# Second graph layer: the input scaling moves from GpSimd to ScalarE, tile by tile, three streams behind the powers

## The chip, the core and the metric

The kernel runs on one core of one Trainium2 chip. The number that counts is the device time in microseconds (us) of one execution. The names of the engines in the rows are PE (TensorE matmul), PEld (TensorE weight load), DVE (VectorE), ACT (ScalarE), POOL (GpSimd) and SP (SyncE, which issues most DMAs).

## What is computed

The input x has 128 graphs of 128 nodes with 128 features, and adj holds a 128 x 128 matrix for each graph. Four blocks follow one another, each added to its own input:

```python
x = x + _L0_gnn_ref(_layernorm(x), adj, ...)    # attention over the graph
x = x + _L0_ffn_ref(_layernorm(x), ...)         # 30 steps: tanh, silu, layernorm, 128x128 product
x = x + _L1_gnn_ref(_layernorm(x), adj, ...)    # relu(f @ W[:d] + (adj @ f) @ W[d:] + bias)
x = x + _L1_ffn_ref(_layernorm(x), ...)         # 8 experts, top 2 of them for each row
```

`_layernorm(x)` is `(x - mean) / sqrt(var + 1e-5)` over the 128 features. The change touches the one in front of the third block, the second graph layer. Its mean is folded into the weights, so that only a multiplication of each row by `1/sqrt(var + eps)` is left.

## The kernel before

The 128 graphs are cut into 16 streams (`STREAMS`) of 8 graphs (`TILES`). A stream's tensor is 128 partitions by 8 tiles by 128 values in float32: `resid[s]` holds what the blocks are added to, `values[s]` (the first 128 columns of `state[s]`) what is being worked on. Every engine has its own program, written out by hand as a software pipeline: in slot k an engine works on stream k of one stage, stream k-1 of the next, and so on. Each engine executes strictly in the order of its program, and semaphores join the engines. No scheduler moves anything.

The 30 steps of the second block run as a loop over 16 slots each. Behind the loop comes its **tail** (`iteration(STEPS, tail=True)`), in which the streams that are still in flight are finished. In slot k of the tail:

- PE transposes a stream (`flip`, L1084), if k is at most 12, and then forms `rows` (L1090 the bias, L1094 the product with `w_ffn`), if k is at most 13. In slot k, `rows` needs the stream that was flipped in slot k-1. The flip of slot k waits for `x2_ready` of k, that is, for DVE's addition in slot k-1, since it writes the PSUM banks which that addition reads.
- ACT copies the stream flipped in slot k-1 out of PSUM into `turned` (L957), and PE's `rows` of slot k waits for this copy.
- DVE adds the product of PE's slot k-2 to `resid[k]` (L691, `x2_ready`), takes the statistics (L661) and writes the variance `x_var` (L665, `x2_var_ready`). DVE has 16 such slots.
- POOL has no part of its own in the tail. Its program goes from the last multiplication of the loop (L515) on to 30 small constant instructions (L524 to L543) and then to the loop over 16 streams at L547 to L552: the power -1/2 of the variance (`rsqrt`, L485, raises `x2_pow`), the multiplication of all 8 tiles by it in one instruction (L550, raises `x2_scaled`), and a copy of row numbers (L552).

Then comes the **second graph layer**, `for k in range(GNN1_SLOTS)` on PE, DVE and ACT. In slot k, PE waits for `x2_scaled` of stream k and flips `values[k]`; it forms the product Q of stream k-1 with `w_mix` (L1094), the mix of stream k-2 (two products for each tile, L1094), flips stream k-4 of the layer's output and forms its router logits (L1213). ACT copies the flip of stream k out (L1021, T below), then the product Q of stream k-1 (L1024), then statistics (L1027) and the flip of stream k-4 (L1032). PE's product Q of stream b waits until ACT has copied out the one of b-1 (`q_copied`). At first POOL has nothing else to do; then it scatters the finished rows to DRAM (L556, 128 indirect DMAs), a stream at a time, when DVE has found their places (L835). The fourth block works on the sorted rows when all are scattered.

Of the kernel before, what the change touches and what calls it, by code (L numbers as in the profile page):

```python
# [10 lines left out]
ALU = mybir.AluOpType  # L11
ACT = mybir.ActivationFunctionType
# [6 lines left out]
def network(nc, x, adj, W_w, W_b, a_w, a_b, ln_w, ln_b, F_W, F_b, G_w, G_b,  # L19
# [4 lines left out]
    TILES = 8  # L24
    STREAMS = B // TILES
    ITERS = 30
    STEPS = STREAMS * ITERS
# [33 lines left out]
    with ExitStack() as ctx:  # L61
        def sb(name, shape, dt=F32):
            return ctx.enter_context(nc.sbuf_tensor(name, shape, dt))

        def sem(name):
            return ctx.enter_context(nc.semaphore(name))
# [27 lines left out]
        resid = [resid_all[:, s] for s in range(STREAMS)]  # L94
        state = [sb(f"state{s}", [P, TILES, ROW]) for s in range(STREAMS)]
        values = [t[:, :, 0:D] for t in state]
# [7 lines left out]
        x_var = [sb(f"x_var{j}", [P, TILES]) for j in range(4)]  # L104
        x_rstd = [sb(f"x_rstd{j}", [P, TILES]) for j in range(4)]
# [8 lines left out]
        minus_half = sb("minus_half", [P, TILES])  # L114
# [150 lines left out]
        x2_pow = sem("x2_pow")  # L265
        x2_scaled = sem("x2_scaled")
# [57 lines left out]
        def wide(v, n=D):  # L324
            return v.unsqueeze(2).to_broadcast([P, v.shape[1], n])

        def halves(v):
            return v.rearrange("p (i h) -> p i h", h=2)

        def of_stats(t, which):  # L330
            return t[:, :, :].rearrange("p i (h e) -> p i h e", h=2)[:, :, :, which]
# [18 lines left out]
        SILU_LAG, STATS_LAG, SCALE_LAG, FLIP_LAG, EVAC_LAG = 1, 2, 5, STREAMS - 3, STREAMS - 2  # L350
        POOL_TILES = 6

        PEEL_FROM, PEEL_EACH = STREAMS + 2, 3
        PEELED = PEEL_EACH * (GNN0_SLOTS - PEEL_FROM)
        Q_LAG, MIX_LAG, X3_LAG, ROWS_LAG, ROUTE_LAG, RANK_LAG, PLACE_LAG = 1, 2, 3, 4, 5, 6, 7
        GNN1_SLOTS = STREAMS + PLACE_LAG
        def not_first(i):
# [5 lines left out]
        def in_flight(k, *lags):  # L363
            return [k - lag if 0 <= k - lag < STREAMS else None for lag in lags]

        def stages(lags, k, base, peeled, tail):
            for lag in lags:
                j = k - lag
                if tail and j >= 0 or peeled and j < 0:
                    yield None, None  # L370
                else:
                    yield base + j, j % STREAMS
# [91 lines left out]
        def _(pool):  # L464
# [19 lines left out]
            def rsqrt(dst, src, done, n):  # L484
                nc.gpsimd.tensor_tensor(dst, src, minus_half[:, 0:src.shape[1]], ALU.pow).then_inc(done, 1)  # L485
                pool.wait_ge(done, n + 1)
# [49 lines left out]
            for low in range(NE - 1):  # L536
# [4 lines left out]
                last = low == NE - 2  # L541
# [3 lines left out]


            for s in range(STREAMS):  # L547
                pool.wait_ge(x2_var_ready, s + 1)
                rsqrt(x_rstd[s % 4][:, :], x_var[s % 4][:, :], x2_pow, s)
                nc.gpsimd.tensor_tensor(values[s], resid[s], wide(x_rstd[s % 4][:, :]), ALU.mult  # L550
                                        ).then_inc(x2_scaled, 1)
                nc.gpsimd.tensor_copy(state[s][:, :, TOKEN].bitcast(I32), ids[:, s * TILES:(s + 1) * TILES])  # L552

            def scatter(s, tiles):
# [8 lines left out]
            for k in range(STREAMS + SCATTER_LAG):  # L563
                s, m = in_flight(k, 0, SCATTER_LAG)
# [44 lines left out]
        def _(dve):  # L609
# [145 lines left out]

            iteration(0, peeled=True, slots=range(PEELED, STREAMS))
            with dve.Fori(STREAMS, STEPS, STREAMS) as q:
# [193 lines left out]
        def _(act):  # L951
            def iteration(base, peeled=False, tail=False, slots=range(STREAMS)):
                for k in slots:
                    (n, s), (l, v) = stages([EVAC_LAG, SILU_LAG], k, base, peeled, tail)
                    if n is not None:
                        act.wait_ge(it_flip, n + 1)
                        nc.scalar.copy(turned[s % 4], ring[s % 4]).then_inc(it_turned, 1)  # L957
                    if peeled:
                        if k >= 4:
                            act.wait_ge(state_read, k - 3)  # L960
                        nc.scalar.activation(turned[k % 4], values[k], ACT.Tanh).then_inc(tanh_done, 1)
                    elif not tail:
                        act.wait_ge(product, base + (k - STREAMS + 1))
                        nc.scalar.activation(values[k], ring[k % 4], ACT.Tanh).then_inc(tanh_done, 1)  # L964
                    if l is not None:
                        act.wait_ge(state_read, l + 1)
                        nc.scalar.activation(values[v], values[v], ACT.Silu).then_inc(silu_done, 1)  # L967
# [37 lines left out]
            act.wait_ge(h0_ready, STREAMS)  # L1005
            iteration(0, peeled=True, slots=range(PEELED, STREAMS))
            with act.Fori(STREAMS, STEPS, STREAMS) as q:
                iteration(q)
            iteration(STEPS, tail=True, slots=range(EVAC_LAG))


            for k in range(GNN1_SLOTS):
                a, b, f, e, r = in_flight(k, 0, Q_LAG, ROWS_LAG, ROUTE_LAG + 1, X3_LAG + 1)
                if e is not None:
                    act.wait_ge(centred_logits, e + 1)
                    nc.scalar.activation(parts[e % 4][:, :, :], parts[e % 4][:, :, :], ACT.Exp).then_inc(exps, 1)
                if a is not None:
                    act.wait_ge(x2_flip, a + 1)
                    if a >= 3:
                        act.wait_ge(mix_psum, a - 2)  # L1020
                    nc.scalar.copy(turned[a % 3], psF).then_inc(x2_turned, 1)  # L1021
                if b is not None:
                    act.wait_ge(q_psum, b + 1)
                    nc.scalar.copy(values[b], psQ).then_inc(q_copied, 1)  # L1024
                if r is not None:
                    act.wait_ge(x3_stats_done, r + 1)
                    nc.scalar.copy(halves(state[r][:, :, MEAN]), of_stats(x1_stats[r % 4], 1)).then_inc(columns_ready, 1)  # L1027
                if f is not None:
                    act.wait_ge(r_flip, f + 1)
                    if f >= 1:  # L1030
                        act.wait_ge(logit_psum, f)
                    nc.scalar.copy(turned[3], psF).then_inc(r_turned, 1)  # L1032
# [281 lines left out]
```

## Time and profile before

| | us |
|---|---|
| median of 3 runs | 2552.14 (2551.59 to 2553.27) |
| the profiled execution, its own time | 2566.49 |
| its span in the trace | 2564.7 |
| busy in it: PE / DVE / ACT / POOL | 2378.7 / 2081.9 / 1811.9 / 2027.5 |
| mean granted clock of TensorE | 0.969 of full speed |

The profiled execution took 14.35 us more than the median of the runs. All times of rows below are of the profiled one, counted from the start of its span. A busy engine is not the same as one that sets the time: the engines wait for one another through semaphores, and only the wait that ends last in a slot matters.

### The profile page before, as it was taken

How to read it: one execution, taken by the hardware profiler on the slowest of the kernel's cores; microseconds unless marked ns; L12 is line 12 of the kernel's file. 1: busy time of each engine (PE TensorE's matmuls, PEld its weight loads, DVE VectorE, ACT ScalarE, POOL GpSimd, SP SyncE). 2: the span in 40 equal slices, each digit the busy share in tenths (PEclk: the TensorE clock that was granted, in tenths of full speed). 3: DMA queues.
4: the chain of work that ended last, by engine and by line, in shares of the span. 5: the costliest groups of instructions: out<-in, count | busy, mean ns of one | idle time of the engine just before them, and what ended most of it. 6: DMA issues, size and time to landing. Idle time of an engine off the chain costs nothing.

```text
span 2564.7 us, 60894 instructions
## 1 busy us (share of the span) xinstructions
PE 2378.7 (93%) x19678; PEld 2320.6 (90%) x19935; DVE 2081.9 (81%) x5761; ACT 1811.9 (71%) x2185; POOL 2027.5 (79%) x1592
## 2 busy tenths in 40 slices
PE   6829999999999999999999999999862999999998
PEld 5829999999999999999999999989861999999998
DVE  5999999999999999999999999987572444444443
ACT  3779999999999999999999999833210334344333
POOL 4769999999999999999999999995764444444443
PEclk9969999999999999999999999999885999999999
DMA  9100000000000000000000000003223555555554
GB/s 261 69 1 1 0 0 0 0 0 0 0 0 0 0 0 0 0 0 0 0 0 0 0 0 0 0 18 110 75 73 109 212 216 212 211 214 216 212 212 148
DMA packets 121574, 164.56 MB, mean 64 GB/s; under 512 B 14982, under 2 KB 74018, under 8 KB 121360
## 3 DMA queue, kind: packets, MB, share of 16 engines
q1 hardware_dynamic: 111792, 145.12, 16.6%
q0 software_dynamic: 9088, 17.14, 2.0%
q10 hardware_dynamic: 608, 1.30, 0.2%
q8 instruction: 37, 0.61, 0.1%
q14 instruction: 49, 0.40, 0.0%
HBM read 40.40 MB, written 24.65 MB: 25 GB/s over the span
## 4 chain that ended last, share of the span: by engine, by line
DVE 58%; PE 31%; issue 7%; POOL 1%; DMA 1%; ACT 1%; SPq 1%; another core or an unknown queue 0%; DVEq 0%; POOLq 0%; ACTq 0%
DVE pair_stats L661 25%; DVE state L704 18%; PE psum L1265 11%; PE psum L1256 11%; DVE state L683 6%; PE psum L1094 5%; PE psum L1084 2%; DVE it_vars L665 2%; DVE x_stats L661 1%; POOL sorted_rows L556 1%; DVE resid L731 1%; PE psum L1213 1%; DMA sorted_rows<-state,slot 1%; PE psum L1246 1%; DVE state L700 1%
## 5 line engine op out<-in xcount | busy, mean ns | idle before, releaser
L1094 PEld LDWEIGHTS psum<-w_ffn,turned 128*128 128x128 f32 x7680 | 1010.1, 192 | 36.0
L1094 PE MATMUL psum<-w_ffn,turned 128*128 128x128 f32 x7680 | 1013.7, 275 | 12.8 <-issue 0.2
L512 POOL TENSOR_TENSOR it_rstd<-it_vars,minus_half 128x8 f32<-128x8 f32 x480 | 785.5, 1636 | 0.0
L515 POOL TENSOR_TENSOR state<-state,it_rstd 128x768 f32<-128x768 f32 x480 | 708.0, 1475 | 37.6
L661 DVE BATCH_NORM_STATS2 pair_stats<-state 128x6 f32<-128x256 f32 x1920 | 685.1, 418 | 0.0
L1084 PE MATMUL psum<-ident,state 128*128 128x128 f32 x4352 | 595.6, 281 | 59.1 <-DVE state L700 42.8
L704 DVE SCALAR_TENSOR_TENSOR state<-state,psum 128x1024 f32<-128x1024 f32 x464 | 560.8, 1209 | 1.8 <-ACT state L964 0.9
L1084 PEld LDWEIGHTS psum<-ident,state 128*128 128x128 f32 x4352 | 479.5, 143 | 78.0 <-issue 57.7
L957 ACT COPY turned<-psum 128x1024 f32<-128x1024 f32 x480 | 485.8, 1012 | 80.4 <-PE psum L1084 43.9
L967 ACT ACTIVATE state<-state 128x1024 f32<-128x1024 f32 x480 | 512.7, 1068 | 28.6 <-DVE state L700 9.1
L964 ACT ACTIVATE state<-psum 128x1024 f32<-128x1024 f32 x464 | 481.0, 1037 | 0.0
L1044 ACT ACTIVATE adjT<-psum 128x512 f32<-128x512 f32 x312 | 186.3, 597 | 283.3 <-PE psum L1256 262.9
L925 DVE TENSOR_TENSOR resid<-psum,adjT 128x128 f32<-128x128 f32 x312 | 91.0, 292 | 305.1 <-PE psum L1265 209.2
L1265 PE MATMUL psum<-resid,adjT 128*128 x2496 | 330.0, 275 | 2.0 <-DVE resid L925 2.0
L1256 PE MATMUL psum<-resid,adjT 128*128 128x128 f32 x2496 | 330.9, 276 | 0.0
L683 DVE TENSOR_SCALAR state<-state,it_rstd 128x128 f32<-128x128 f32 x960 | 318.5, 372 | 0.0
L1265 PEld LDWEIGHTS psum<-resid,adjT 128*128 128x128 f32 x2496 | 303.6, 192 | 2.6 <-issue 2.4
L1256 PEld LDWEIGHTS psum<-resid,adjT 128*128 128x128 f32 x2496 | 304.8, 193 | 0.0
L1090 PE MATMUL psum<-bias_mv,ones_bf 128*128 128x512 bf16 x736 | 279.7, 380 | 0.0
L596 POOL DMA_INDIRECT out_dram<-resid,adjT x156 | 161.1, 1033 | 129.0 <-DVE resid L930 96.7
L591 POOL TENSOR_TENSOR row_scale<-adjT,minus_half 128x1 f32<-128x1 f32 x156 | 89.3, 572 | 208.6 <-DMA adjT<-sorted_rows 205.5
L556 POOL DMA_INDIRECT sorted_rows<-state,slot x128 | 125.3, 979 | 81.7 <-issue 37.1
(190 smaller groups left out, 1725.2 us busy)
## 6 DMA issues: line engine op xcount, KB each, us to landing
adjT<-resid SPq DMA_DIRECT2D x312, 320.0 KB
adjT<-sorted_rows SPq DMA_DIRECT2D x156, 66.5 KB, 1.8
resid<-in_x_dram SPq DMA_DIRECT2D x16, 512.0 KB, 7.3
state<-in_adj_dram SPq DMA_DIRECT2D x16, 512.0 KB, 7.3
adjT_dram<-adjT SPq DMA_DIRECT2D x7, 512.0 KB, 3.7
adjT<-adjT_dram SPq DMA_DIRECT2D x7, 512.0 KB, 3.5
out_dram<-resid,adjT POOLq DMA_INDIRECT x156, 2.4
sorted_rows<-state,slot POOLq DMA_INDIRECT x128
```

The lines of the kernel that those rows point to most:

```text
L512: nc.gpsimd.tensor_tensor(it_rstd[s % 8][:, :], it_vars[s % 4][:, :], minus_half[:, 0:TILES], ALU.pow).then_inc(it_pow, 1)
L515: nc.gpsimd.tensor_tensor(values[s][:, 0:POOL_TILES, :], values[s][:, 0:POOL_TILES, :], wide(it_rstd[s % 8][:, 0:POOL_TILES]), ALU.mult).t ...
L661: last = nc.vector.bn_stats(dst[:, i, :], src[:, 2 * i:2 * i + 2, :].rearrange("p t d -> p d t"))
L683: last = nc.vector.tensor_scalar(values[r][:, t, :], values[r][:, t, :], it_rstd[r % 8][:, t:t + 1], None, ALU.mult)
L704: nc.vector.scalar_tensor_tensor(values[k], values[k], 0.01, ring[k % 4], ALU.mult, ALU.add).then_inc(state_read, 1)
L957: nc.scalar.copy(turned[s % 4], ring[s % 4]).then_inc(it_turned, 1)
L964: nc.scalar.activation(values[k], ring[k % 4], ACT.Tanh).then_inc(tanh_done, 1)
L967: nc.scalar.activation(values[v], values[v], ACT.Silu).then_inc(silu_done, 1)
L1084: last = nc.tensor.transpose(dst[:, t, :], src[:, t, :], ident[:, :])
L1094: last = nc.tensor.matmul(dst[:, t, :], stationary(t), moving(t), start=bias is None and m == 0, stop=m == len(terms) - 1, skip_group_chec ...
L1256: last = nc.tensor.matmul(psH[o % 4][:, c, :], w1[:, c * P:(c + 1) * P], turned_T[o // 2 % 4], start=True, stop=True)
L1265: last = nc.tensor.matmul(psY[o % 2], hidden[o % 4][:, c, :], w2_all[:, bass.ds(e, 1), c, :].rearrange("p o d -> p (o d)"), start=c == 0, ...
```

## The change

GpSimd keeps the powers and the copies of row numbers. The multiplication goes to ScalarE, as eight ACTIVATE instructions for each stream (one for each tile, with the tile's column of `x_rstd` as the scale). They are placed behind the copy out of slot k = s+3 of the tail for the streams 0 to 10, and between the copies T and Q of the layer's slots 0 to 4 for the streams 11 to 15. `x_rstd` has four buffers, so GpSimd's power of stream s waits from s = 4 on until stream s-4 is scaled.

```diff
@@ GpSimd
             for s in range(STREAMS):
+                if s >= 4:
+                    pool.wait_ge(x2_scaled, s - 3)
                 pool.wait_ge(x2_var_ready, s + 1)
-                rsqrt(x_rstd[s % 4][:, :], x_var[s % 4][:, :], x2_pow, s)
-                nc.gpsimd.tensor_tensor(values[s], resid[s], wide(x_rstd[s % 4][:, :]), ALU.mult
-                                        ).then_inc(x2_scaled, 1)
+                nc.gpsimd.tensor_tensor(x_rstd[s % 4][:, :], x_var[s % 4][:, :], minus_half[:, :], ALU.pow
+                                        ).then_inc(x2_pow, 1)
                 nc.gpsimd.tensor_copy(state[s][:, :, TOKEN].bitcast(I32), ids[:, s * TILES:(s + 1) * TILES])
@@ ScalarE
-            iteration(STEPS, tail=True, slots=range(EVAC_LAG))
+            def scale_inputs(s):
+                act.wait_ge(x2_pow, s + 1)
+                for t in range(TILES):
+                    last = nc.scalar.activation(values[s][:, t, :], resid[s][:, t, :], ACT.Copy,
+                                                scale=x_rstd[s % 4][:, t:t + 1])
+                last.then_inc(x2_scaled, 1)
+
+            for k in range(EVAC_LAG):
+                iteration(STEPS, tail=True, slots=range(k, k + 1))
+                if k >= X2_LAG:
+                    scale_inputs(k - X2_LAG)
 
 
             for k in range(GNN1_SLOTS):
@@
                     nc.scalar.copy(turned[a % 3], psF).then_inc(x2_turned, 1)
+                if k < STREAMS - EVAC_LAG + X2_LAG:
+                    scale_inputs(k + EVAC_LAG - X2_LAG)
                 if b is not None:
```

Here `X2_LAG` is 3 and `EVAC_LAG` is 14.

What stands in the engines' programs is shown at two places. The first is ACT's program from the last copy of the loop into the tail, before the change. The thirteen copies from PSUM to `turned` are those of the tail's slots 1 to 13, and the next line opens the graph layer.

```order
L957 COPY turned<-psum 128x1024 [waits it_flip]
L967 ACTIVATE state15<-state15 128x8x128 [waits state_read]
L957 COPY turned<-psum 128x1024 [waits it_flip] x13
L1021 COPY turned<-psum 128x1024 [waits x2_flip] x2
L1024 COPY state0<-psum 128x8x128 [waits q_psum]
```

Now the same place reads so (the line numbers are three higher for the same code; L1015 is the new line):

```order
L960 COPY turned<-psum 128x1024 [waits it_flip] x3
L1015 ACTIVATE state0<-resid,x_rstd0 128x128 [waits x2_pow]
L1015 ACTIVATE state0<-resid,x_rstd0 128x128 x7
L960 COPY turned<-psum 128x1024 [waits it_flip]
L1015 ACTIVATE state1<-resid,x_rstd1 128x128 [waits x2_pow]
L1015 ACTIVATE state1<-resid,x_rstd1 128x128 x7
L960 COPY turned<-psum 128x1024 [waits it_flip]
L1015 ACTIVATE state2<-resid,x_rstd2 128x128 [waits x2_pow]
```

The copy of slot 4 now stands behind the scaling of stream 0, and so on to slot 13. A little further, at the entry to the graph layer:

```order
L1034 COPY turned<-psum 128x1024 [waits x2_flip]
L1015 ACTIVATE state11<-resid,x_rstd3 128x128 [waits x2_pow]
L1015 ACTIVATE state11<-resid,x_rstd3 128x128 x7
L1034 COPY turned<-psum 128x1024 [waits x2_flip]
L1015 ACTIVATE state12<-resid,x_rstd0 128x128 [waits x2_pow]
L1015 ACTIVATE state12<-resid,x_rstd0 128x128 x7
L1039 COPY state0<-psum 128x8x128 [waits q_psum]
```

The two copies T that stood together are now eight instructions apart, and as many stand between T of slot 1 and the first copy Q.

The second place is POOL's program from the last of its constants on, before:

```order
L543 MEMSET pair_steps 128x1
L485 TENSOR_TENSOR x_rstd0<-x_var0,minus_half 128x8 [waits x2_var_ready]
L550 TENSOR_TENSOR state0<-resid,x_rstd0 128x8x128 [waits x2_pow]
L552 COPY state0<-ids 128x8
L485 TENSOR_TENSOR x_rstd1<-x_var1,minus_half 128x8 [waits x2_var_ready]
```

And now:

```order
L545 MEMSET pair_steps 128x1
L553 TENSOR_TENSOR x_rstd0<-x_var0,minus_half 128x8 [waits x2_var_ready]
L555 COPY state0<-ids 128x8
L553 TENSOR_TENSOR x_rstd1<-x_var1,minus_half 128x8 [waits x2_var_ready]
L555 COPY state1<-ids 128x8
```

Only the multiplications are gone. The first power keeps its place behind the loop's work and the constants.

## Rows read from the trace of the kernel before

**Rows 1.** The page, section 4: the chain that ended last, by engine.
```profile
DVE 58%; PE 31%; issue 7%; POOL 1%; DMA 1%; ACT 1%; SPq 1%; another core or an unknown queue 0%; DVEq 0%; POOLq 0%; ACTq 0%
```

**Rows 2.** Busy time by stretch: PE, PEld, DVE, ACT, POOL, clock, DMA, GB/s.
```profile
1680.00:1700.00 20.00, 17.34 (x138) 16.10 (x140) 19.62 (x33) 5.06 (x5) 19.53 (x17) 1.00 0.00 1
...
1740.00:1760.00 20.00, 19.89 (x182) 19.85 (x183) 14.38 (x57) 6.29 (x9) 5.92 (x6) 1.00 0.19 63
1760.00:1780.00 20.00, 16.84 (x127) 16.41 (x128) 10.59 (x47) 4.07 (x7) 14.79 (x14) 0.84 0.30 82
```

**Rows 3.** Timeline of POOL: start, length, instruction, idle before it.
```profile
1657.61 1.64 POOL L512 TENSOR_TENSOR it_rstd<-it_vars,minus_half 128x8 f32<-128x8 f32 x1
...
1672.37 1.63 POOL L485 TENSOR_TENSOR x_rstd<-x_var,minus_half 128x8 f32<-128x8 f32 x1
1674.07 1.90 POOL L550 TENSOR_TENSOR state<-resid,x_rstd 128x1024 f32<-128x1024 f32 x1
...
1677.79 1.90 POOL L550 TENSOR_TENSOR state<-resid,x_rstd 128x1024 f32<-128x1024 f32 x1
```

**Rows 4.** Timeline of DVE in the tail: its variances.
```profile
1657.85 0.16 DVE L665 TENSOR_SCALAR it_vars<-pair_stats 128x8 f32<-128x8 f32 x1
...
1671.62 0.17 DVE L665 TENSOR_SCALAR x_var<-x_stats 128x8 f32<-128x8 f32 x1
...
1678.62 1.09 DVE L665 TENSOR_SCALAR x_var<-x_stats 128x8 f32<-128x8 f32 x1
```

**Rows 5.** Timeline of PE in the tail and into the layer.
```profile
1670.27 1.06 PE L1084 MATMUL psum<-ident,state 128*128 128x128 f32 x8
...
1680.98 1.06 PE L1084 MATMUL psum<-ident,state 128*128 128x128 f32 x8 [0.43 <-DVE resid L691]
1681.88 0.38 PE L1090 MATMUL psum<-bias_mv,ones_bf 128*128 128x512 bf16 x1
...
1702.61 0.38 PE L1090 MATMUL psum<-bias_mv,ones_bf 128*128 128x512 bf16 x1
...
1704.82 1.04 PE L1084 MATMUL psum<-ident,state 128*128 128x128 f32 x8
...
1711.10 2.46 PE L1094 MATMUL psum<-w_mix,turned 128*128 128x128 f32 x18 [0.32 <-ACT state L1024]
...
1731.15 1.85 PE L1213 MATMUL psum<-wr_c,turned 128*128 128x8 f32 x16
```

**Rows 6.** Timeline of ACT in the tail and into the layer.
```profile
1665.00 1.01 ACT L957 COPY turned<-psum 128x1024 f32<-128x1024 f32 x1 [3.60 <-PE psum L1084]
...
1700.60 1.01 ACT L957 COPY turned<-psum 128x1024 f32<-128x1024 f32 x1 [2.69 <-PE psum L1084]
1705.89 1.01 ACT L1021 COPY turned<-psum 128x1024 f32<-128x1024 f32 x1 [4.29 <-PE psum L1084]
...
1709.94 1.02 ACT L1024 COPY state<-psum 128x1024 f32<-128x1024 f32 x1 [0.77 <-PE psum L1094]
```

**Rows 7.** Groups of ACT by shape: busy us, mean ns, idle before.
```profile
L972 ACT ACTIVATE state<-resid,shift,x_rstd 128x128 f32<-128x128 f32 x128 | 51.0, 483 | 2.9 <-POOL shift L506 2.9
L1049 ACT ACTIVATE resid<-psum 128x128 f32<-128x128 f32 x156 | 43.2, 277 | 114.0 <-PE psum L1246 64.6 <-issue 49.4
```

**Rows 8.** Timeline of ACT in the first layer: eight tiles in a row.
```profile
55.44 3.19 ACT L972 ACTIVATE state<-resid,shift,x_rstd 128x128 f32<-128x128 f32 x8
```

**Rows 9.** Timeline of PE at the end of the first layer.
```profile
136.77 2.02 PE L1131 MATMUL psum<-state,adjT 128*128 128x129 f32 x16 [1.32 <-DVE resid L731]
142.34 3.58 PE L1131 MATMUL psum<-state,adjT 128*128 128x129 f32 x16 [3.55 <-DVE resid L731]
```

**Rows 10.** Timeline of POOL: the first scatter.
```profile
1754.79 1.21 POOL L556 DMA_INDIRECT sorted_rows<-state,slot  x1 [9.48 <-DVE slot L835]
```

**Rows 11.** Waits from 1640 to 2000: total, times, longest.
```profile
POOL sorted_rows L556 <- DVE slot L835: 25.2, 7, 9.5
```

**Rows 12.** The chain that ended last, in order of time: the last scatter.
```profile
1957.53 3.23 DMA sorted_rows<-state,slot
```

More of the change, by code:

```diff
@@ L354, in network @@
         PEELED = PEEL_EACH * (GNN0_SLOTS - PEEL_FROM)
+        X2_LAG = 3
         Q_LAG, MIX_LAG, X3_LAG, ROWS_LAG, ROUTE_LAG, RANK_LAG, PLACE_LAG = 1, 2, 3, 4, 5, 6, 7
```

## The prediction

> **What bounds the kernel now.** I read the page's chain first: DVE 58%, PE 31%, ACT and POOL 1% each [rows 1]. For a change in one stage that average says little, so I went to the stretches around 1655 to 1760 us. From 1680 to 1700, the tail, DVE and POOL are both busy for over 19.5 of 20 us, PE for 17.34, ACT for 5.06 [rows 2]. Two full engines side by side ask which one drives the other, and the timelines answer it. POOL's rhythm is one stream in 3.72 us (1674.07 to 1677.79) [rows 3]. DVE's variance of a stream takes 0.17 us while POOL does not yet multiply, but 1.09 us later, from 1678.62 to 1679.71, and POOL's multiplication ends at 1677.79 + 1.90 = 1679.69 [rows 3, 4]. So DVE is held until that multiplication ends, its next addition comes late, and PE's flip waits for that addition: 0.43 us idle before the flip [rows 5]. The Trainium skill states such a lock (SBUF — State Buffer, section SBUF: two separate sides): GpSimd and VectorE share one pair of ports, whoever starts first holds it for the whole instruction. This trace agrees, for the multiplication (1.09 instead of 0.17 us).
>
> The tail thus runs at POOL's pace, about 3.7 us a slot. Without the lock the next limit is PE: a flip takes 0.90 us to the next start (1680.98 to 1681.88), `rows` 2.21 (1702.61 to 1704.82), 3.11 together [rows 5]. In the graph layer PE is full, 19.89 of 20 us [rows 2]. From the first scatter at 1754.79 on, POOL and PE take turns until the last one lands at 1957.53 + 3.23 = 1960.76 [rows 10, 12]; the first scatter waited for its places 9.48 us, so its start follows PE and DVE of this layer, and a shift of PE's whole sequence there shifts the end.
>
> **Step 1, what goes.** 16 multiplications of 1.90 us leave POOL, and with them the hold on DVE. PE's slots can shrink from 3.7 to 3.11 us. Alone, over the 8 slots from 5 to 12 that run at the slow pace, that could give some 8 x 0.59 = 4.7 us.
>
> **Step 2, when the first power comes.** It is the step that decides. POOL's first power starts at 1672.37 and ends at 1674.00 [rows 3]. It stands behind POOL's own backlog of the loop and the constants, none of which changes, and its input had long been ready. But ACT's scaling of stream 0 stands right behind the copy of slot 3, which starts at 1665.00 and ends at 1666.01 [rows 6]. ACT executes in order, so it waits there for 1674.00 - 1666.01 = 8.0 us. Queued behind it is the copy of slot 4, and for that copy waits PE's `rows` of slot 4, which before started right behind the flip, at 1670.27 + 0.90 = 1671.17 [rows 5]. POOL's and DVE's work up to there does not depend on this copy, so nothing brings the power forward.
>
> **Step 3, what a scaled stream costs ACT.** No such instruction (a column as scale, a constant bias) is in the trace. From below: 277 ns for a 128-column ACTIVATE with neither scale nor bias column [rows 7]. From above: 483 ns for one with both [rows 7]. Eight of the latter take 3.19 us together, so they start (3.19 - 0.483) / 7 = 0.387 us apart, 0.096 less than their length [rows 8]. The start-to-start distance is then between 0.181 and 0.387. The new one has one of two columns, so I take the middle of 0.300 (the lower row is read from PSUM; for SBUF I allow some 0.02 more) and 0.483, that is 0.390 long and 0.294 apart: 2.35 us a stream. The Trainium skill gives for this (ScalarE: Activation LUTs, section What ACT_TABLE_LOAD costs) 186 ns plus 0.833 ns a column plus 93 ns for each pointer operand, overlapping by 93: an estimate from that page is 0.293 apart, and the sum would be the same within 0.1 us.
>
> **Step 4, the tail.** The scaling of stream 0 starts at about 1674.1 and is through at 1676.45. The copy of slot 4 then runs to 1677.45, and `rows` of slot 4 starts at 1677.6 (an engine starts about 0.15 us after what it waited for ends). That is 6.4 us later than before. From there ACT repeats copy (0.91 to the next start) and scaling (2.35), 3.26 us a slot, more than PE's 3.11. ACT is now the pace. The copy of slot 13 comes at 1676.45 + 9 x 3.26 = 1705.8, `rows` of slot 13 at 1706.95, and the first flip of the graph layer at 1706.95 + 2.21 = 1709.2. Before it was at 1704.82 [rows 5]: **+4.35 us**. So of the 6.4 lost, 2.05 come back.
>
> **Step 5, the entry to the graph layer.** Counting from that first flip, before: the copy T0 at 1.07, and PE's second product Q at 1711.10 - 1704.82 = 6.28, right behind ACT's first copy Q (1709.94 + 1.02) [rows 5, 6]. Now: T0 at 1.07; scaling of stream 11 from 1.98 to 4.33; T1, ready at 3.33, from 4.33 on; scaling of stream 12 from 5.24 to 7.59; the first copy Q, whose product is ready at 5.1, from 7.59 to 8.61; PE's second product Q at 8.75. **+2.47 us.** Later slots have a mix on PE and are long enough: in slot 4, the last with a scaling, the last copy of ACT ends at about 27.7, and the logits that wait for it stood at 1731.15 - 1704.82 = 26.33 before [rows 5], so stand at 28.8 now. Nothing more is added, and nothing comes back, because PE is full from there on [rows 2].
>
> **Step 6, POOL and DVE.** POOL has 3.72 - 1.90 = 1.82 us a stream left (power and copy) [rows 3] and waits for ACT from stream 4 on. That wait costs nothing: by step 4 scaling s ends at 1676.45 + 3.26 s, and the power of s+4 is wanted by ACT four slots later. DVE's slot of 3.72 was full; with 0.17 for the held 1.09 it has 2.8 us of work, and waits for PE. ACT's added 16 x 2.35 = 38 us lie in its idle time but for what steps 4 and 5 count.
>
> **Step 7, the clock.** PE idles from about 1671 to 1677.6 with only a flip before. At the end of the first layer 16 matmuls took 2.02 us, and after 3.55 us of idle time the same 16 took 3.58 [rows 9], near the ratio of 1.2 to 2.4 GHz. From 1760 to 1780 the mean clock is 0.84, which is 0.16 x 2 x 20 = 6.4 us at half [rows 2]. As much here loses up to 3.2 us of PE, a part of it while PE is still idle; of the rest the slots take back 0.15 each, 1.2 in all. Between 0 and 1.6 us remain; I take 0.2.
>
> **The sum.** 4.35 + 2.47 + 0.2 = **+7.0 us**. The profiled execution would take 2566.5 + 7.0 = 2573.5. It lay 14.35 us above the median of the runs; nothing in the steps hangs on the profiling, so I carry the difference over: 2552.1 + 7.0 = **2559.1 us**, +0.27%. What this measurement can tell from no change is about 0.2%, 5.1 us.
>
> **The rivals.**
> - *Cheap tiles* (0.17): the distance is nearer to 0.181. Then a stream costs 1.45, ACT's slot 2.36, and PE's 3.11 is the pace. Stream 0 is through at 1675.55, `rows` of slot 4 at 1676.7, and with 8 slots of 3.11 and a last one of 2.21 the layer's first flip comes at 1706.0, +1.2; the entry adds 0.67. +1.9, 2554.0 us. The limit between this and the forecast, +5.1, is at 0.276. For it speaks only that the scale column may be free.
> - *Dear tiles* (0.06): 0.387. A slot of ACT is 4.0 us, more than the old pace: +11.8, and +3.95 at the entry. +15.8, 2567.9 us.
> - *The first power holds nobody* (0.06): were it there at 1666, or the delay hidden, the same 3.26 us slots from the copy at 1665.00 on put slot 13's copy at 1697.6 instead of 1700.60 [rows 6] and the layer's first flip at 1701.0, 3.85 early; with the +2.47 that is -1.4, 2550.7 us. Against it stand the rows of step 2.
> - *The power holds DVE* (0.03): a power takes 1.64 us and would hold the variance as the multiplication did. DVE's slot would be up to 3.72 - 1.09 + 1.64 = 4.3 us, over ACT's 3.26, in 9 slots: +9.5 more, +16.5, 2568.6 us. The row speaks against it: a variance at 1657.85 took 0.16 us within the power that began at 1657.61 [rows 3, 4]. The rule named above, an exclusive hold for every GpSimd instruction, would say this.
> - *Faster* (0.09): POOL waits for the places of rows in 25.2 us at 7 scatters, 9.5 of it before the first [rows 11]. The other 15.7 come from PE's interrupted matmuls and its low clock from 1760 on [rows 2]. If the shifted meeting of scatters and PE took them away, all of them, the result is 7.0 - 15.7 = -8.7, 2543.4 us; it decides from 12.1 of the 15.7 on. Nothing in the change touches their cause, so it would be luck.
>
> **How the numbers follow.** The forecast case (first power late, one-column price, +5.1 to +10) has 0.59. Slower by over 0.2%: 0.59 + 0.06 + 0.03 = 0.68. Within 0.2%: cheap tiles 0.17 + nobody held 0.06 = 0.23. Faster: 0.09. The range reaches from just under the case in which the power holds nobody, 2550.5, to 2566.0, which takes in the forecast with a longer time at the low clock and half of the way to the dear tiles; outside are 0.09 + 0.03 + 0.05 = 0.17. The forecast case's own range is 2557.3 to 2562.
>
> **What the profile after would show.** Step 1: variances of 0.17 us in the tail. Step 2: one idle time of about 8 us on ACT before the first tile, released by POOL's power at about 1674, and PE idle for some 6 us before `rows` of slot 4, released by ACT. Step 3: tiles of 390 ns, eight in about 2.45 us. Step 4: ACT's copies 3.26 us apart, each tile group right behind its copy, first flip of the layer at about 1709. Step 5: second product Q 8.75 us after it. Step 6: first scatter at about 1761.6. The prediction is wrong if the power comes before ACT is there, if the tiles are much cheaper than 0.276 us apart, or if POOL's waits after the first scatter add up to something other than 15.7 us.

## The result and the profile after

The changed kernel took 2558.95 us (median of 8 runs, 2557.22 to 2559.85), the kernel before 2550.28 (8 runs, 2549.86 to 2553.27) on the same chip: +8.7 us, a ratio of 1.0031 with a 95% interval of 1.0020 to 1.0042. A second group of runs gave 2560.29 against 2551.22, 1.0032 (1.0020 to 1.0044). The forecast was 2559.1.

The profiled execution of the changed kernel took 2558.14 us, with a span of 2556.3. Line numbers are three higher on ACT and DVE and 15 higher on PE (L1084 is L1099, L1094 is L1109). The timeline of ACT after the change, from the copy of slot 3 on:

```profile
1663.84 1.01 ACT L960 COPY turned<-psum 128x1024 f32<-128x1024 f32 x1 [3.60 <-PE psum L1099]
1672.88 2.45 ACT L1015 ACTIVATE state<-resid,x_rstd 128x128 f32<-128x128 f32 x8 [8.02 <-POOL x_rstd L553]
1675.22 0.99 ACT L960 COPY turned<-psum 128x1024 f32<-128x1024 f32 x1
1676.12 2.45 ACT L1015 ACTIVATE state<-resid,x_rstd 128x128 f32<-128x128 f32 x8
1678.46 1.00 ACT L960 COPY turned<-psum 128x1024 f32<-128x1024 f32 x1
...
1708.78 1.01 ACT L1034 COPY turned<-psum 128x1024 f32<-128x1024 f32 x1 [1.00 <-PE psum L1099]
1709.69 2.44 ACT L1015 ACTIVATE state<-resid,x_rstd 128x128 f32<-128x128 f32 x8
1712.03 0.99 ACT L1034 COPY turned<-psum 128x1024 f32<-128x1024 f32 x1
1712.92 2.45 ACT L1015 ACTIVATE state<-resid,x_rstd 128x128 f32<-128x128 f32 x8
1715.27 1.00 ACT L1039 COPY state<-psum 128x1024 f32<-128x1024 f32 x1
```

These answer to [rows 6]. ACT stands 8.02 us in front of the first scaled tile, released by POOL's power. The copy of slot 4, which came 3.19 us after that of slot 3, now comes 11.38 us after it. From there copies are 3.24 us apart with no idle time between: ACT sets the pace. In the layer two blocks of scaling stand between the copies, and the first copy Q is late. The timeline of PE over the same time answers to [rows 5]:

```profile
1669.12 1.07 PE L1099 MATMUL psum<-ident,state 128*128 128x128 f32 x8
1676.28 0.61 PE L1105 MATMUL psum<-bias_mv,ones_bf 128*128 128x512 bf16 x1 [6.09 <-ACT turned L960]
1676.68 1.92 PE L1109 MATMUL psum<-w_ffn,turned 128*128 128x128 f32 x8
...
1707.70 1.04 PE L1099 MATMUL psum<-ident,state 128*128 128x128 f32 x8
1709.93 1.06 PE L1099 MATMUL psum<-ident,state 128*128 128x128 f32 x8 [1.19 <-ACT turned L1034]
...
1713.17 1.06 PE L1099 MATMUL psum<-ident,state 128*128 128x128 f32 x8 [0.38 <-ACT turned L1034]
1716.42 3.40 PE L1109 MATMUL psum<-w_mix,turned 128*128 128x128 f32 x16 [2.18 <-ACT state L1039]
```

PE idles 6.09 us before `rows` of slot 4, and these then take 3.64 us (1676.28 to the next flip at 1679.92) instead of 2.21. The layer's first flip comes 1707.70 - 1663.84 = 43.86 us after ACT's copy of slot 3; before it was 1704.82 - 1665.00 = 39.82. PE's second product Q is 8.72 us behind that flip instead of 6.28, and its 16 matmuls take 3.40 us. Busy time by stretch says why (PE, PEld, DVE, ACT, POOL, clock, DMA, GB/s):

```profile
1668.00:1676.00 8.00, 2.18 (x18) 1.85 (x16) 7.83 (x19) 3.12 (x9) 7.93 (x36) 0.78 0.00 0
1676.00:1680.00 4.00, 3.73 (x19) 3.49 (x20) 0.62 (x3) 4.00 (x13) 4.00 (x7) 0.59 0.01 4
1680.00:1684.00 4.00, 4.00 (x36) 3.91 (x35) 3.62 (x7) 4.00 (x13) 2.51 (x3) 1.00 0.00 0
1712.00:1716.00 4.00, 1.85 (x16) 1.45 (x14) 0.00 (x0) 4.00 (x11) 1.78 (x2) 1.00 0.00 0
1716.00:1720.00 4.00, 3.58 (x17) 3.50 (x18) 0.00 (x0) 3.67 (x11) 0.00 (x0) 0.60 0.02 4
```

The granted clock fell from 2.4 to 1.2 GHz twice: around the long idle time in the tail, and again behind the idle times of the entry (1.19, 0.38 and 2.18 us). A stretch that shows 0.59 or 0.60 was for the most part at 1.2 GHz. Before the change the entry has idle times of 1.19 and 0.32 us.

POOL and DVE, where the powers and the variances meet (timeline, after; they answer to [rows 3, 4]):

```profile
1671.21 1.63 POOL L553 TENSOR_TENSOR x_rstd<-x_var,minus_half 128x8 f32<-128x8 f32 x1
...
1672.95 1.64 POOL L553 TENSOR_TENSOR x_rstd<-x_var,minus_half 128x8 f32<-128x8 f32 x1
```
```profile
1673.65 0.17 DVE L668 TENSOR_SCALAR x_var<-x_stats 128x8 f32<-128x8 f32 x1
```

With no multiplication on POOL the variance takes 0.17 us again, although it lies within a power.

### The profile page after: what moved, and what is told of

Same layout as the page of the kernel before. It is cut to its first block, busy times and chain, and to the rows that moved or that the text cites. A ratio compares the mean times of both kernels' runs of the same rounds, so it can differ in the third digit from the quotient of the medians.

```text
span 2556.3 us, 61274 instructions
## 1 busy us (share of the span) xinstructions
PE 2379.1 (93%) x19934; PEld 2308.7 (90%) x19935; DVE 2071.8 (81%) x5761; ACT 1848.8 (72%) x2313; POOL 2000.5 (78%) x1576
## 4 chain that ended last, share of the span: by engine, by line
POOL 58%; PE 29%; DVE 5%; issue 4%; ACT 2%; DMA 1%; POOLq 1%; SPq 1%; DVEq 0%
POOL it_rstd L514 30%; POOL state L517 26%; PE psum L1280 11%; PE psum L1271 11%; PE psum L1109 3%; POOL sorted_rows L559 2%; PE psum L1099 1%; DVE resid L734 1%; ACT state L1015 1%; PE psum L1228 1%; DVE x_stats L664 1%; PE psum L1261 1%; DVE pair_stats L664 1%; DMA sorted_rows<-state,slot 1%; POOLq L513 1%
## 5 line engine op out<-in xcount | busy, mean ns | idle before, releaser
L1109 PEld LDWEIGHTS psum<-w_ffn,turned 128*128 128x128 f32 x7680 | 1010.9, 192 | 36.2
L1109 PE MATMUL psum<-w_ffn,turned 128*128 128x128 f32 x7680 | 1014.2, 275 | 0.0
L1099 PE MATMUL psum<-ident,state 128*128 128x128 f32 x4352 | 592.2, 280 | 56.2 <-DVE state L703 42.6
L1099 PEld LDWEIGHTS psum<-ident,state 128*128 128x128 f32 x4352 | 476.3, 142 | 74.5 <-issue 54.0
L1105 PE MATMUL psum<-bias_mv,ones_bf 128*128 128x512 bf16 x992 | 377.7, 381 | 14.5 <-DVE state L782 7.7
```

The costliest lines, as they stand in the source:

```text
L1099: last = nc.tensor.transpose(dst[:, t, :], src[:, t, :], ident[:, :])
L1105: nc.tensor.matmul(dst[:, 4 * bank:4 * bank + 4, :], ones_bf[:, :], bias_mv[bias][:, :, :], start=True, stop=False, skip_group_check=True)
L1109: last = nc.tensor.matmul(dst[:, t, :], stationary(t), moving(t), start=bias is None and m == 0, stop=m == len(terms) - 1, skip_group_chec ...
```

## The experiments

To compare kernels I take points in each trace relative to ACT's copy of slot 3 (1665.00 before, 1663.84 after), since all work up to it is the same. "Flip" is the first flip of the graph layer, "Q" PE's second product Q behind that flip, "scatter" the start of the first scatter, "phase" the time from the start of the first to that of the last scatter. (Rows 12 and the prediction call the scatter at 1957.53 the last one. It is not: in that trace the last one starts at 1971.72 and lands at 1974.03.) The phase is read for each trace from its own last scatter. Time is the median of 11 runs (8 and 6 for the changed kernel), "before" that of the kernel before on the same chip (8 to 33 runs). The intervals are those of the ratio to it.

| kernel | flip | Q | scatter | phase | time | before | ratio, interval |
|---|---|---|---|---|---|---|---|
| before, first profile | 39.8 | 6.3 | 89.8 | 216.9 | 2566.5 (one) | | |
| before again | 39.8 | 6.3 | 89.8 | 201.8 | 2549.9 (one) | 2550.9 | |
| changed | 43.9 | 8.7 | 97.9 | 202.3 | 2558.95 | 2550.28 | 1.0031 (1.0020, 1.0042) |
| changed again | 43.9 | 8.7 | 97.9 | 203.0 | 2560.29 | 2551.22 | 1.0032 (1.0020, 1.0044) |
| six behind | 35.6 | 8.7 | 89.6 | 202.6 | 2551.42 | 2550.90 | 0.9998 (0.9989, 1.0007) |
| behind the copy Q | 43.9 | 6.4 | 93.9 | 202.1 | 2555.39 | 2550.90 | 1.0016 (1.0007, 1.0025) |
| no wait for the power | 35.7 | 8.7 | 88.2 | 202.6 | 2550.40 | 2550.90 | 0.9997 (0.9988, 1.0006) |
| constants later | 41.8 | 8.7 | 95.8 | 210.1 | 2567.67 | 2562.71 | 1.0024 (1.0015, 1.0033) |
| no multiplication | 35.4 | 6.3 | 85.4 | 211.1 | 2560.81 | 2562.71 | 0.9992 (0.9983, 1.0001) |
| the same again | 35.4 | 6.3 | 85.4 | 202.2 | 2546.65 | 2551.22 | 0.9981 (0.9972, 0.9990) |
| constant scale | 42.6 | 7.2 | 93.5 | 214.1 | 2566.39 | 2562.71 | 1.0015 (1.0006, 1.0024) |
| six behind, end of slot | 35.6 | 6.4 | 85.6 | 213.9 | 2557.69 | 2562.71 | 0.9986 (0.9977, 0.9995) |
| the same again | 35.6 | 6.4 | 85.6 | 200.9 | 2547.38 | 2551.22 | 0.9983 (0.9974, 0.9992) |
| and a tile on DVE | 35.4 | 6.4 | 85.5 | 202.6 | 2547.18 | 2551.22 | 0.9983 (0.9974, 0.9992) |

**The kernel before once more** (no edit). 

> The kernel before, profiled once more, because its first profile (2566.5 us) lay 14 to 16 us over its timed runs while the one of the changed kernel (2558.1) lay on its own. Theory: the first profile caught an outlier, with interrupted matmuls between the first and the last scatter; the new one has a time near 2550.3 us and a scatter phase near the 202.2 us that the changed kernel shows (1761.75 to 1964.0), not 217. The tail looks as before: slots of 3.70 us, layer's first flip 39.8 us after the copy of slot 3. Rival: the scatter phase is shorter after the change because of the change, so before shows about 217 us again and about 2566 us.

It took 2549.94 us with a phase of 201.8, so the first profile was the odd one. Its longer phase is not the work of profiling: the waits of this trace, from 1640 to 2000, answer to [rows 11].

```profile
POOL sorted_rows L556 <- DVE slot L835: 11.0, 6, 9.5
```

Only 1.5 us of waits for places are left behind the first one, where the first profile had 15.7. That trace also had PE idle on "issue" between single matmuls (L1094, 5.7 us at 10 places, from 1760 to 1975); this one has none of that on L1094.

**Six instead of three streams behind.**

```diff
-        X2_LAG = 3
+        X2_LAG = 6
```


> The changed kernel with the scaling six instead of three streams behind. Theory (ACT stands 8.0 us in front of the first power, then paces the tail at 3.24 us a slot): the scaling of stream 0 now follows the copy of slot 6, which starts 9.6 us after that of slot 3, when the power is there; no idle time on ACT from it, and the layer's first flip comes about 35.8 us after the copy of slot 3 (39.8 before, 43.9 after the change). The entry still costs 2.4 us, or 4.1 if the clock falls there again. Time: 2550.3 - 4.0 + 2.4 (+1.6) = 2548.7 to 2550.4 us. Rival (the pace of ACT, not the wait, costs the time): the number of scaled tiles is the same, so it stays within 2 us of 2559.

The timeline of ACT:

```profile
1664.99 1.01 ACT L960 COPY turned<-psum 128x1024 f32<-128x1024 f32 x1 [3.60 <-PE psum L1099]
...
1674.56 1.01 ACT L960 COPY turned<-psum 128x1024 f32<-128x1024 f32 x1 [2.18 <-PE psum L1099]
1675.47 2.45 ACT L1015 ACTIVATE state<-resid,x_rstd 128x128 f32<-128x128 f32 x8
1677.82 0.99 ACT L960 COPY turned<-psum 128x1024 f32<-128x1024 f32 x1
```

No idle time stands in front of the first tile. The flip comes 8.3 us sooner than after the change, the first scatter 8.3 sooner, and the time is that of before within its interval: +0.5 us, where 2548.7 to 2550.4 against 2550.3, that is -1.6 to +0.1, was expected; the first scatter shows -0.2. The rival, that the tiles themselves cost the time, would have left it near 2559 and is out. The edit also moves three streams out of the tail: streams 8 to 15 are now scaled in the layer's slots 0 to 7. That this is not what gives the time back is shown two experiments further on, where all eleven stay in the tail and the flip comes at 35.7.

**The scaling behind the copy Q.**

```diff
-                if k < STREAMS - EVAC_LAG + X2_LAG:
-                    scale_inputs(k + EVAC_LAG - X2_LAG)
                 if b is not None:
                     act.wait_ge(q_psum, b + 1)
                     nc.scalar.copy(values[b], psQ).then_inc(q_copied, 1)
+                if k < STREAMS - EVAC_LAG + X2_LAG:
+                    scale_inputs(k + EVAC_LAG - X2_LAG)
```


> The changed kernel with the scaling of streams 11 to 15 behind the copy Q of the slot instead of in front of it. Theory: the tail is untouched (layer's first flip 43.9 us after the copy of slot 3), PE's second product Q comes 6.4 us after that flip instead of 8.7 and its idle time of 2.2 us there goes, so the clock does not fall: 2.3 + 1.6 us less, 2555.0 us. Rival (the product Q is late since ACT is late from the tail, whatever the order): 2559, unchanged.

The timeline of PE shows the second product Q with no wait before it, and at the full clock:

```profile
1708.70 1.04 PE L1099 MATMUL psum<-ident,state 128*128 128x128 f32 x8
...
1715.08 2.46 PE L1109 MATMUL psum<-w_mix,turned 128*128 128x128 f32 x18
```

The tail is that of the changed kernel (flip at 43.9), Q at 6.38, and the first scatter 4.0 us sooner: 2.3 us of the order and 1.6 of the clock. The time, 2555.39, is 4.5 over before.

**The same tiles without the wait for the power.**

```diff
-                act.wait_ge(x2_pow, s + 1)
+                act.wait_ge(x2_ready, s + 1)
...
-                                                scale=x_rstd[s % 4][:, t:t + 1])
+                                                scale=minus_half[:, t:t + 1])
```


> The changed kernel, but ACT multiplies by a constant column instead of the reciprocal root, and waits for DVE's addition of the stream instead of for the power: the same 128 instructions at the same places, without the wait for GpSimd. Its output is not the reference's. Theory: the 8.0 us of idle time on ACT go, the copies stay 3.24 us apart, and the layer's first flip comes some 36 us after the copy of slot 3. Time 2550.3 - 3.9 + 2.4 (+1.6) = 2548.8 to 2550.5 us. Rival (ACT's work itself is the cost): between 2555 and 2559 us.

The timeline of ACT:

```profile
1664.74 1.01 ACT L960 COPY turned<-psum 128x1024 f32<-128x1024 f32 x1 [3.60 <-PE psum L1099]
1665.65 2.45 ACT L1015 ACTIVATE state<-resid,minus_half 128x128 f32<-128x128 f32 x8
1668.00 1.00 ACT L960 COPY turned<-psum 128x1024 f32<-128x1024 f32 x1
```

The same instructions at the same places, and the flip comes at 35.7 instead of 43.9. That is the direct test of step 2: the wait for the first power costs 8.1 us of the tail, and without it ACT's pace would leave the tail 4.1 us shorter than before. Q is still 8.7 behind, yet here its matmuls take 2.46 us, and the next product Q is 15.45 us behind the flip instead of 17.09: PE has the same three idle times at the entry as in the changed kernel, and the clock did not fall. The timeline of PE:

```profile
1709.20 2.46 PE L1109 MATMUL psum<-w_mix,turned 128*128 128x128 f32 x18 [2.18 <-ACT state L1039]
```

So the first scatter is 1.6 us before the one of before, and the time is the same within the interval.

**The constants behind the powers.** The block from `first = 0` to `done.then_inc(pair_tables, 1)` on GpSimd stands behind the loop of powers instead of in front of it, nothing else. 

> The changed kernel with GpSimd's 30 constant instructions moved behind its loop of powers. Theory: the first power comes 2.1 us sooner, and so does all that hangs on it: ACT's idle time is 5.9 instead of 8.0 us, PE's 4.0 instead of 6.1, the layer's first flip 41.8 us after the copy of slot 3; the clock may fall less. Time 2559.0 - 2.1 = 2556.9 us, or up to 1 us less. Rival (the first power's date doesn't matter): 2559, unchanged.

The timeline of ACT, and then of PE:

```profile
1672.62 2.45 ACT L1015 ACTIVATE state<-resid,x_rstd 128x128 f32<-128x128 f32 x8 [5.96 <-POOL x_rstd L529]
```
```profile
1676.02 0.39 PE L1105 MATMUL psum<-bias_mv,ones_bf 128*128 128x512 bf16 x1 [4.01 <-ACT turned L960]
```

Both waits shrank by the 2.1 us that the power came sooner, the flip by the same, the first scatter by 2.1. In this group of runs the kernel before took 2562.71 us as well, and against it this one had +5.0 us where 2556.9 - 2550.3 = 6.6 was expected; the interval, 3.8 to 8.5, holds both.

**No multiplication at all.** On GpSimd the `tensor_tensor` with `ALU.mult` is left out of the kernel before, and the copy of row numbers raises `x2_scaled`. 

> The kernel before without any multiplication of the layer's inputs, on no engine: GpSimd does the powers and the copies of row numbers, which now release PE. Its output is not the reference's. Theory (the multiplications hold DVE's variance and so set 3.70 us a slot): DVE's variances take 0.17 us, slots are 3.1 us, the layer's first flip comes some 35.5 us after the copy of slot 3 instead of 39.8. Time 2550.3 - 4.3 = 2546.0 us. Rival (GpSimd's multiplications hold nobody, DVE is as slow by itself): 2550, unchanged.

The timeline of DVE:

```profile
1677.02 1.43 DVE L660 BATCH_NORM_STATS2 x_stats<-resid 128x6 f32<-128x256 f32 x4
1678.47 0.17 DVE L664 TENSOR_SCALAR x_var<-x_stats 128x8 f32<-128x8 f32 x1
1678.56 1.22 DVE L690 TENSOR_TENSOR resid<-psum,resid 128x1024 f32<-128x1024 f32 x1
```

The variance takes 0.17 us in every slot, and its slots are 2.8 us of work. The flip comes at 35.4, 4.4 sooner than before, and the first scatter 4.4 sooner. The time fell by only 1.9 us, and its interval reaches from 4.4 less to 0.3 more, so I ran it again. 

> The kernel before without any multiplication of the layer's inputs, once more: its first scatter came 4.5 us sooner than before, but its time was 1.9 us less with an interval from 0.0 to 4.4. Its output is not the reference's. Theory: 4.4 us less. Rival (with other values the scatter phase takes longer): 2 us less, with a scatter phase over 2 us longer than that of the kernels that route as before.

Now it was 4.6 us less, with a phase of 202.2. So the longer phase of 211.1 does not come from the other values; the kernels with the right values had 210.1 and 213.9 in the same group of runs.

**A number as the scale.** `scale=0.5` instead of the column, waits kept. 

> The changed kernel with the number 0.5 as the scale of the 128 ACTIVATE instructions instead of the column, all waits kept. Its output is not the reference's. It measures the price of the column and shows what a cheaper tile is worth. Theory: a tile takes about 0.30 instead of 0.39 us, eight in 1.7 instead of 2.45, and a slot of ACT 2.5 us, so that PE's 3.1 is the pace. The 8.0 us in front of the first power stay. The layer's first flip comes 41.2 us after the copy of slot 3, PE's second product Q 7.3 us behind it: 2550.3 + 2.3 = 2552.6 us, up to 2 more if the clock falls at the entry. Rival (the wait for the power is all, the tile's price nothing): 2559.

The groups of ACT by shape (busy us, mean ns, idle before), of this kernel and of the changed one:

```profile
L1015 ACT ACTIVATE state<-resid 128x128 f32<-128x128 f32 x128 | 27.3, 300 | 8.0 <-POOL x_rstd L553 8.0
```
```profile
L1015 ACT ACTIVATE state<-resid,x_rstd 128x128 f32<-128x128 f32 x128 | 39.3, 404 | 8.0 <-POOL x_rstd L553 8.0
```

The column costs 104 ns a tile; eight take 1.71 instead of 2.45 us. With the cheaper tile the flip comes at 42.6, not at the expected 41.2, and Q at 7.23 as expected. I had counted with a full clock behind the idle time. Here `rows` of slot 4 takes 3.99 us (1677.92 to the next flip at 1681.91) instead of 2.21, at a granted clock of 0.50 from 1676 to 1680. In the changed kernel ACT's copies follow one another without a gap up to slot 13, so that PE's slow `rows` of slot 4 delays nobody. With the cheaper tile PE sets the pace, and those 1.8 us are in the flip in full: the start of these `rows` at 11.69, 3.99 for them, eight slots of 3.09 and 2.21 for the last `rows` add up to 42.6. Time +3.7 us, 3.7 by the first scatter.

**Both costs taken away:** six streams behind, and `scale_inputs` as the last thing in ACT's slot of the layer. 

> The changed kernel with the scaling six streams behind, and in the graph layer at the end of ACT's slot, behind both copies. It leaves out what the theory holds to be the two costs. Theory: no idle time of ACT in front of a scaling, first flip of the layer 35.8 us after the copy of slot 3, second product Q 6.4 us behind it as before the change: 2550.3 - 4.0 + 0.1 = 2546.4 us, faster than both kernels. Rival (added work on ACT in the graph layer's full slots delays the logits): 2549 or more.

It was 5.0 us faster than before, by the first scatter 4.2. Once more: 

> The kernel with the scaling six behind and at the end of the slot, once more, beside the one above that moves a tile to VectorE. Theory: 4.1 us less than before by its landmarks (first scatter 85.7 us after the copy of slot 3 instead of 89.8); it had 5.0 less. Rival: no difference that can be told.

3.8 us faster, 0.9983 (0.9974 to 0.9992). This version beats the kernel before in both groups, and the changed kernel in the one in which that ran too (2547.38 against 2560.29 us). The fuller slots of the layer do not show as a delay: its first scatter comes 4.2 us sooner than in the kernel before, and so does its flip, to 0.1 us.

**One tile of the tail's streams on VectorE** in addition, between its statistics and its variance:

```diff
+                        j = k - X2_LAG
+                        if 0 <= j < SHARED:
+                            dve.wait_ge(x2_pow, j + 1)
+                            nc.vector.tensor_scalar(values[j][:, TILES - 1, :], resid[j][:, TILES - 1, :],
+                                                    x_rstd[j % 4][:, TILES - 1:TILES], None, ALU.mult
+                                                    ).then_inc(x_scaled, 1)
```
Left out of this cut: ACT then scales seven tiles of these streams instead of eight, and GpSimd's powers and PE's flips wait for VectorE's tile too.

> The kernel with the scaling six behind and at the end of the slot, but VectorE scales the last of the 8 tiles of streams 0 to 7 in the tail. Theory: ACT's slot becomes 0.90 + 7 x 0.29 = 2.95 us instead of 3.24 and VectorE's 2.8 + 0.2 = 3.0, so PE's 3.09 sets the pace from slot 7 to 12: the layer's first flip comes 34.7 to 35.0 us after the copy of slot 3 instead of 35.6. Time 0.6 to 0.9 us below the kernel without it, which is at the limit of what can be told. Rival (a further wait between engines costs what it gives): 35.6 or more.

The timeline of ACT:

```profile
1675.85 2.16 ACT L1022 ACTIVATE state<-resid,x_rstd 128x128 f32<-128x128 f32 x7
1678.02 1.01 ACT L967 COPY turned<-psum 128x1024 f32<-128x1024 f32 x1
1678.93 2.16 ACT L1022 ACTIVATE state<-resid,x_rstd 128x128 f32<-128x128 f32 x7
1681.11 1.01 ACT L967 COPY turned<-psum 128x1024 f32<-128x1024 f32 x1
```

ACT's copies are 3.09 us apart, PE's pace, as meant. But the flip comes at 35.4, only 0.2 sooner, where 34.7 to 35.0 was expected, and the time is the same as without. Without any multiplication it is 35.4 too, with the same pace of 3.09 us, so that is PE's own floor. ACT's copy of slot 13 came 31.2 us after that of slot 3 instead of 32.3, but `rows` of slot 13 has no flip in front of it, and with ACT as the pace PE had made up for most of the difference there.

## Why the prediction was right

**Step 1, held.** Without multiplications on POOL the variance takes 0.17 us and the flip comes 4.4 us sooner. The forecast was 4.7, from eight slow slots of 0.59 us each; before the change only seven distances between ACT's copies, from slot 6 to slot 13, are 3.7 us or more.

**Step 2, held, and it decides.** ACT's idle time was 8.02 us against 8.0, and PE's `rows` of slot 4 start 6.3 us late, against 6.4. Without this wait the tail is 8.1 us shorter with the same tiles, and a power 2.1 us sooner gives 2.1 us.

**Step 3, held.** Eight tiles take 2.45 us, (2.45 - 0.404) / 7 = 0.292 apart, against 0.294. A tile's mean is 404 ns, against 390, and the row of the constant scale gives the part of the column.

**Step 4, held, 0.3 us too dear.** ACT's slot is 3.24 instead of 3.26 us, the flip +4.04 instead of +4.35.

**Step 5, held.** +2.44 against +2.47, and putting the scaling behind the copy gives back 2.3.

**Step 6, held in what it costs.** ACT waits for POOL only once, the 8.0 us. But POOL does not wait for ACT from stream 4 on, as was said: it waits eight times for DVE's variance (10.6 us in all) and for ACT's tiles only twice (3.9 us).

**Step 7 is the term that was mis-sized.** I looked for the low clock only behind the long idle time and took 0.2 us. There it fell and cost nothing: PE's slow `rows` of slot 4 ran from 1676.28 to about 1679.9, while ACT's pace left room. It fell again at the entry, behind three short idle times, and cost 1.6 us. The first of them stood there before the change too; the other two come from the late copies that step 5 had itself worked out, and the step did not ask what they do to the clock. PE's first logits of the router stand 74.27 us after the copy of slot 3 instead of 66.15, 8.12 later, and 8.12 - 4.04 - 2.44 = 1.64. In the kernel with the copy first, the idle time of 2.18 us is gone and so are the 1.6 us. The stretch from 1760 to 1780, from which the step took its upper bound, was no usual one either: its clock of 0.84 is 1.00 when the kernel before is profiled again.

The sum by the trace is then +8.1 us at the first scatter (97.9 - 89.8), against +7.0. The runs show +8.7 and +9.1, with intervals of 5.1 to 10.7 and 5.1 to 11.2; what they have beyond 8.1 is less than they can tell. That the forecast of 2559.1 lies within 0.2 us of the measured 2558.95 is luck: the added 7.0 us are 1.7 less than the measured difference, and the median that they were added to (2552.1 from three runs) is 1.9 above the one from eight (2550.3).

**The step from the profiled execution to the median** came out right for a reason that was not the one given. I took the first profile's 14.35 us over the median as something that would stay a property of profiled executions. It was a longer phase of scatters in that one execution, 216.9 against 201.8 us; other profiled executions take what timed ones do. The rival "faster" was built on the 15.7 us of waits in the same phase, which a usual execution does not have: its price was wrong, not only its chance. This is also the one sign of being wrong that came true. The prediction said that it is wrong if POOL's waits after the first scatter add up to something other than 15.7 us. After the change the waits from 1640 to 2000 are these:

```profile
POOL sorted_rows L559 <- DVE slot L838: 11.3, 7, 9.5
```

That leaves 1.8 us, and 1.5 in the kernel before profiled again. What failed is the premise that the first profile stands for all executions, not the working of the tail and the entry.

**The rivals.** Cheap and dear tiles: out, since the tiles start 0.292 us apart, over the limit of 0.276 and far from 0.387. The cheap rival's price was too low besides: with the number as the scale tiles start 0.20 us apart, and the time is +3.7 us, where the rival had +1.9. It left out the 1.8 us that the slow `rows` of slot 4 cost when PE sets the pace. The first power holds nobody: out for this kernel, but made true by an edit it gives the forecast -1.4 us within the interval (-0.5 us by the runs, -1.6 by the first scatter). The power holds DVE: out; variances within a power take 0.17 us. The rule of the Trainium skill that was weighed there (SBUF — State Buffer, section SBUF: two separate sides), that a GpSimd instruction holds the shared ports for its whole length, agrees with the multiplications of 1.90 us (the variance takes 1.09 us and ends with them) and differs from these traces for the powers of 1.64 us (0.17 us within them); the measurement decides.

## What to carry to other kernels

When work moves to an engine that executes in order, look first at when its input is ready, and at what stands behind it in the queue. The input here came from an instruction that had always been late. In the kernel before nothing in the tail waited for it but GpSimd, the engine that was late itself. The new work wants a place at which its input is old, and in a slot the place behind everything that others wait for: the same 128 instructions cost 8 to 9 us at one place and gave back 4 at another.

## What the runs showed of the hardware

Short idle times can cost the clock, and not always. With the same three idle times at the entry (1.19, 0.38 or 0.39, and 2.18 us) the second product Q or the mix behind it ran at the lower level (1.2 GHz) in the traces of the changed kernel (both), of the one six behind and of the one with the constants later, 1.6 us each, and at 2.4 GHz in the trace without the wait for the power. With a number as the scale the last idle time is 1.28 us, and the clock stayed at 2.4 GHz. What decides between them these runs do not show.

The phase of the scatters took 201 to 203 us in some groups of runs and 210 to 214 in the group where the kernel before took 2562.71 us, with the same program, and 216.9 in the first profile. Such traces have idle time named "issue" between single matmuls of PE. I have not found out where it comes from; the three groups of experiments ran on three different chips, one each, so that the chip and the group cannot be told apart. The landmarks ahead of the phase agree to 0.1 us in all groups, and so tell more than the medians of kernels from different groups.
